# Low one-hots of a group's six chunks in two fixed buffers, in place of a ring addressed by register

## What is computed

```python
# layer 0: relational messages, summed by target node
Z = h @ W_shared.T; ze = he @ W_shared.T
a = Z[src] @ Wa_s.T + ze @ Wa_e.T + Z[dst] @ Wa_d.T
H_all = jnp.einsum('ni,rio->nro', h, W_rel)
out = relu(segment_sum(H_all[src, rel] * a, dst, N_NODES))
# layer 1 (twice) and layer 2 (four times): sums over the same edges
h = segment_sum(x[src], dst, num_nodes)
# layer 3: edge features summed by src, then an MLP
```

## Time and profile before

| what | us |
|---|---|
| median of 3 runs | 4683.87 (4682.92 to 4687.05) |
| the profiled execution, first to last instruction | 6104.5 |
| group stage in the profiled execution | about 226 to 3024 |
| from there to the end | about 3080 |

### The profile page before, as it was taken

The page is one execution under the profiler, slowest core; times in us unless marked ns, Lnnn a source line. Parts: engine busy times, 40 slices in busy tenths (PEclk is TensorE's granted clock), DMA queues, the critical chain, the costliest instruction groups (busy, mean ns, idle before and its releaser), DMA issues.

```text
span 6104.5 us, 83728 instructions
## 1 busy us (share of the span) xinstructions
PE 3504.6 (57%) x18191; PEld 1755.8 (29%) x18192; DVE 2563.8 (42%) x7891; ACT 1503.7 (25%) x3741; POOL 3187.4 (52%) x3191
## 2 busy tenths in 40 slices
PE   5377777777777777776324544345365345455347
PEld 2133333333333333333101222112132112222136
DVE  6266666666666666666330020131120021120368
ACT  3133333323323232322211111111111112111158
POOL 2455555555555555555376555645625635626720
PEclk8588888878888887888656676667666667667679
DMA  5333333333333333333123444334324334324256
GB/s 181 93 77 81 81 78 78 77 80 77 77 77 80 77 77 78 80 77 71 38 93 135 145 146 131 119 112 145 107 79 144 111 132 146 108 79 156 79 200 237
DMA packets 593641, 646.86 MB, mean 106 GB/s; under 512 B 423668, under 2 KB 430418, under 8 KB 587261
## 3 DMA queue, kind: packets, MB, share of 16 engines
q1 hardware_dynamic: 374705, 459.40, 23.2%
q0 software_dynamic: 101760, 110.75, 9.2%
q10 hardware_dynamic: 117068, 75.50, 4.1%
HBM read 451.74 MB, written 190.23 MB: 105 GB/s over the span
## 4 chain that ended last, share of the span: by engine, by line
PE 35%; issue 21%; another core or an unknown queue 21%; DVE 10%; DMA 8%; ACT 2%; POOL 2%; DVEq 1%; SPq 0%; ACTq 0%; POOLq 0%
PE bank L1742 10%; PE bank L1743 7%; PE bank L1823 6%; PE bank L1747 6%; DMA ld_all<-adjacency 3%; DMA rel_table<-ld_all 2%; DMA rel_and_z<-adjacency 1%; DVE hid_T L1305 1%; DMA ld_all<-l_sorted 1%; POOL l_sorted L711 1%; DVE hid_T L1326 1%; DVE hid_T L1584 1%; PE bank L1939 1%; PE bank L1771 1%
## 5 line engine op out<-in xcount | busy, mean ns | idle before, releaser
L711 POOL DMA_INDIRECT l_sorted<-arena,l_pos x1504 | 1539.2, 1023 | 1339.3 <-ACT arena L854 877.4
L686 POOL DMA_INDIRECT ld_all<-rel_table,rel_and_z x1564 | 1545.8, 988 | 1133.0 <-remote 503.2
L1742 PE MATMUL bank<-hid_T 128*128 128x400 f16 x2346 | 965.7, 412 | 672.6 <-issue 539.8
L1743 PE MATMUL bank<-hid_T 128*128 128x384 f16 x2346 | 940.5, 401 | 44.3 <-issue 43.5
L1326 DVE TENSOR_SCALAR hid_T<-count_key,hid_T 128x400 f16<-128x400 int16 x2346 | 592.1, 322 | 754.5 <-remote 526.7
L1823 PE MATMUL bank<-rel_and_z,ld_all 128*128 128x512 fp8e4 (+1 forms) x1872 | 522.3, 414 | 602.9 <-issue 534.1
L1823 PE MATMUL bank<-ld_all 128*128 128x512 fp8e4 (+1 forms) x1950 | 511.4, 420 | 337.4 <-issue 138.4
L1747 PE MATMUL bank<-ld_all,arena 128*32 x4692 | 527.1, 250 | 123.3 <-issue 121.3
L1742 PEld LDWEIGHTS bank<-hid_T 128*128 x2346 | 255.9, 109 | 1157.3 <-issue 1153.9
L774 ACT CAST ld_all<-bank 128x400 fp8e4<-128x400 f32 x391 | 191.1, 489 | 1551.6 <-remote 999.7
L1266 DVE COPY accT<-bank 128x512 f32<-128x512 f32 (+1 forms) x78 | 51.1, 656 | 1215.4 <-remote 797.1
(11 more groups left out here) (289 smaller groups left out, 4103.0 us busy)
## 6 DMA issues: line engine op xcount, KB each, us to landing
ld_all<-adjacency SPq DMA_DIRECT2D x72, 1600.0 KB
rel_and_z<-adjacency SPq DMA_DIRECT2D x72, 1600.0 KB
l_sorted<-zeros SPq DMA_DIRECT2D x147, 424.0 KB
arena<-in_edge_attr SPq DMA_DIRECT2D x195, 256.0 KB
ld_all<-l_sorted SPq DMA_DIRECT2D x33, 1277.5 KB, 6.0
adjacency<-ld_all ACTq DMA_DIRECT2D x391, 100.0 KB
rel_table<-ld_all SPq DMA_DIRECT2D x49, 520.0 KB, 3.6
ld_all<-rel_table,rel_and_z POOLq DMA_INDIRECT x1564
```

The costliest lines, as they stand in the source:

```text
L686: pool.indirect_dma_start(ring[:, c % RING, 0:TW], None, rel_table, bass.IndirectOffsetOnAxis(ap=rel_i[:, c:c + 1], axis=0)).then_inc(s(f" ...
L711: pool.indirect_dma_start(l3_sorted, bass.IndirectOffsetOnAxis(ap=l3_pos[0:parts, n * SB_K + k:n * SB_K + k + 1], axis=0), rows16[q][0:par ...
L1742: pe.matmul(b0[:, 0:w0], low[:, 0:P], pair_hot[q % 2][:, k, 0:w0], start=k == 0, stop=k == CG - 1)
L1743: pe.matmul(b1[:, 0:GW - w0], low[:, P:2 * P], pair_hot[q % 2][:, k, 0:GW - w0], start=k == 0, stop=k == CG - 1)
```

## The change

The ring goes. Two tiles `low_hot[0..1]` of six chunks each, and two small tiles of six keys each (`low_in`), take its place in `hid_T`. For each group DVE copies the six keys from `lo_key` at the group's first chunk (`low_keys`, an `also`, issued ahead of `pair_keys`), and makes six low one-hots from them (`low_hots`). PE takes `low_hot[q % 2][:, k, :]`, whose address is fixed when the program is compiled. The copy of 32 keys in each turn of the loop, the three rounds made ahead of the loop and the copy ahead of the tail go. The last three groups get low one-hots too, and their placeholder instruction is a memset of another tile.

```diff
-        lo_ring = hid_T[:, at:at + LO_RING * P].bitcast(f16).rearrange("p (c f) -> p c f", c=LO_RING)
-        assert at + LO_RING * P <= NP
+        low_hot, low_in = [], []
+        for q in range(2):
+            low_hot.append(hid_T[:, at:at + CG * P].bitcast(f16).rearrange("p (c f) -> p c f", c=CG))
+            at += CG * P
+            low_in.append(hid_T[:, at:at + CG])
+            at += CG
...
-                def low_hots(r, q, k0):
+                def low_keys(q, first):
+                    return v.tensor_copy(low_in[q % 2], lo_key[:, bass.ds(first, CG)])
+
+                def low_hots(q):
 
-                    for k in range(K):
-                        v.tensor_scalar(lo_ring[:, q * K + k, :], io256[:], lo_in[:, k0 + k:k0 + k + 1], None, ALU.is_equal)
+                    for k in range(CG):
+                        v.tensor_scalar(low_hot[q % 2][:, k, :], io256[:], low_in[q % 2][:, k:k + 1], None, ALU.is_equal)
...
-                link(v.tensor_copy(lo_in[:, 0:LAG * K], lo_key[:, 0:LAG * K]))
                 for r in range(LAG):
-                    low_hots(r, r, r * K)
                     link(add_source_term(r, r // 2, r % 2))
-                with fast.over(NG // TG, 2 + 4 + 2 * TG - 1 + 8) as b:
+                with fast.over(NG // TG, 2 + 4 + 3 * TG - 2 + 8) as b:
                     first = first_of(b * TG)
-                    fast.also(v.tensor_copy(lo_in, lo_key[:, bass.ds(b * (TG * K) + LAG * K, TG * K)]))
+                    fast.also(low_keys(0, first))
...
-                        low_hots(r, r % TG, q * K)
+                        low_hots(q)
...
+                            fast.also(low_keys(q + 1, coming))
                             link(pair_keys(g + 1, q + 1, coming))
...
                 for k in range(CG):
-                    low = lo_ring[:, bass.ds((first + k) & (LO_RING - 1), 1), :].rearrange("p a f -> p (a f)")
+                    low = low_hot[q % 2][:, k, :]
```

More of the change, by code:

```diff
@@ L294, in build @@
             at += CG
-        lo_ring = hid_T[:, at:at + LO_RING * P].bitcast(f16).rearrange("p (c f) -> p c f", c=LO_RING)
-        assert at + LO_RING * P <= NP
+        low_hot, low_in = [], []
[4 more added lines that the diff above has]
+            at += CG
+        assert at <= NP
         count_bank = [(4, 5), (0, 1)]
@@ L1396, in _ @@
                     positions(b)
-                link(v.tensor_copy(lo_in[:, 0:K * (ROUNDS % TG)], lo_key[:, ROUNDS // TG * TG * K + LAG * K:ROUNDS // TG * TG * K + LAG * K + K * (ROUNDS % TG)]))
                 v.wait_ge(s("he_loaded3"), 16 * (PIECES // 4) + 32)
@@ L1404, in _ @@
                     first = first_of(g)
+                    fast.also(low_keys(q, first))
                     link(pair_keys(g, q, first))
@@ L1407, in _ @@
                     row_hots(g, q, first)
+                    low_hots(q)
                     if r < ROUNDS:
-                        low_hots(r, r % TG, q * K)
                         link(add_source_term(r, r // 2, r % 2))
                     else:
-                        link(v.memset(lo_in[:, 0:1], 0))
+                        link(v.memset(over_sum[:], 0))
                     row_weights(q, first)
```

## The result

| | us | runs |
|---|---|---|
| before | 4683.4 (4680.37 to 4687.05) | 4 |
| after | 4911.6 (4908.57 to 4914.0) | 4 |

The ratio is 1.0488, 95% interval 1.0473 to 1.0503: the change makes the kernel 228 us slower. The forecast was 4657, in a range of 4590 to 4760. The result lies 152 us above its upper end, and no rival had named the cause.

What follows compares the result with a forecast made beforehand. PE's sequencer was taken to bind the group stage at 5.28 us a group; with DVE at 5.19 and POOL at 5.2 the pace becomes 5.21, so 391 x 0.07 = 27 us off 4683.87 gives 4657, range 4590 to 4760.

Steps and rivals of the forecast that it cites:

- DVE's turn: DVE's loop over eight groups: the turn itself takes 1.6 us, from the idle 1.07 ahead of L1370 to the first L1326.
- PE at 5.28 before: Group stage before the change: PE needs 5.28 us a group and its sequencer binds, read from a full-clock stretch.
- PE's chunks without addresses: PE at L1742: six chunks save 0.135 us each, 0.8 a group, and then follow each other by 0.33.
- DVE at 5.19: DVE in the group stage: two more one-hots and a key copy raise 4.74 to 5.19 us a group, between 5.1 and 5.3.
- POOL: POOL's gathers in the group stage: keep 5.0 to 5.2 us a group; six one-hots add 0.03 to 0.05; its wait vanishes.
- rival D: The port: each added one-hot holds POOL back for its whole 0.197 us, round 5.6, 125 us slower, 4809; 5%.
- Rival A: Group stage: PE's pace before was under 5.17, so DVE's 5.19 binds after; 74 or 35 us slower, 4758 or 4719; 27%.
- B: Group stage: POOL sets the pace before and after at 5.2, 0 to 9 us either way, 4684; 20%.
- C: Group stage: DVE and POOL are cheaper in a run, PE is not; 5.28 to 5.0, 109 us faster, 4575; 10%.
- The clock: PE's granted clock in the group stage: falling to half in places costs 0 to 15 us; taken as 0.
- The profiled span of 5450 to 5600: Profile after: with less PE sequencer work under the profiler, the span falls 500 to 660 us from 6104.5.
- Whole arrival: Group stage to end: later stages start behind it and POOL's long scatter is unchanged, so a gain there arrives whole.

Runs made afterwards that it cites:

- merged: The changed kernel with pair and low keys made by one instruction, so 287 instructions in a turn of DVE's loop in place of 303: 4652.1 us.
- merged_pad16: `merged` with 16 one-column memsets of an unused tile put into DVE's loop, 303 instructions a turn again: 4908.5 us.
- before_again: The kernel before, unchanged, profiled once more: a span of 4677.7 us, against 6104.5 in the first profile.
- pe_fixed: The kernel before with a fixed address for PE's low one-hots and DVE untouched, so the wrong chunks are read: 4666.2 us.
- full_unroll: The changed kernel with all 48 turns of DVE's loop written out, so no jump: 4629.4 us.
- pad16: The kernel before with 16 one-column memsets of an unused tile added to DVE's loop, 289 instructions a turn: 4671.4 us.
- two_turns: The changed kernel with DVE's loop body written twice, 24 turns of sixteen groups in place of 48 of eight: 4741.0 us.
- merged_unroll: `merged` with all turns of DVE's loop written out: 4656.3 us.
- before_unroll: The kernel before with DVE's loop of eight-group turns written out 48 times: 4679.9 us.

## Why the prediction was wrong

**The step that failed** is DVE's turn. The prediction carried it over unchanged ("the turn itself, from the idle 1.07 ahead of L1370 to the first L1326, 1.6") and said "No wait is added". It priced the added instructions by their execution and not by their place in the program. The term was 1.07 and became 6.43 a turn. 48 x 5.34 = 256 us, of which 28 are hidden or gained elsewhere; 228 were measured. No edit of the diff is the cause by itself: 16 memsets in the loop do it to `merged` (`merged_pad16`), and 32 ahead of it to the kernel before.

**PE at 5.28 before: right**, though read from an odd execution. A group takes 5.29 in `before_again`, PE is busy for 866 of 1000 us there at a clock of 0.97, and its weight loads at L1742 wait 380.6 us for "issue" in 1000. The stretch at full clock in the earlier trace rows was indeed what a run looks like.

**PE's chunks without addresses: right.** In after, timeline of PE at full clock:

```profile
1519.51 0.34 PE L1749 MATMUL bank<-hid_T 128*128 128x400 f16 x1 [1.17 <-DVE arena L1343]
1519.69 0.33 PE L1750 MATMUL bank<-hid_T 128*128 128x384 f16 x1
1519.85 0.33 PE L1749 MATMUL bank<-hid_T 128*128 128x400 f16 x1
```

Chunks follow each other by 0.34, against 0.49 and 0.46 in the earlier trace rows. What this is worth is another matter: `pe_fixed` has it alone, and gains 14 us.

**DVE at 5.19: near**, as what is left without the stall. 5.92 less 5.34 / 8 is 5.25, within the 5.1 to 5.3 of the prediction. `full_unroll`, which has no turn, makes a group in 5.18, and `merged`, which has no key copy, in 1000 / 192 = 5.21; DVE sets the groups' pace in both. `merged` takes 4652, close to the forecast of 4657, but that is in part luck: the forecast turns DVE's pace of 5.21 into time, and in `merged` POOL's gathers and scatters run through without a wait and set when the long scatter starts. The prediction had POOL's total (2113) and PE's (2114) a microsecond apart, so it saw how near POOL was.

**POOL: right.** Its round of 5.0 to 5.2 is the next bound in `pe_fixed`, and is 5.20 in `before_again`, 5.15 in `merged` and 5.10 in `full_unroll` from first to last gather. Six one-hots in place of four didn't slow a gather: 966 ns on average after, and 978 in `before_again`. POOL's wait for PE did not vanish, though; it grew to the 78.8 us shown above. The round of 5.10 to 5.15 with six one-hots excludes rival D's 5.6, and with it what the rule on the port in the Trainium skill's page SBUF — State Buffer, section "Who interferes with whom", gives when it is taken to the letter. Rival A's mechanism, PE's pace in a run under 5.17, is excluded by the 5.29. B and C named no loss of this size and fall with the result.

**The clock: right that it costs nothing here.** It falls from 0.97 to 0.86, as PE has waited longer between groups, and some groups go at 1.2 GHz: after the stall of 1498 us PE has waited 9.53 us, and its chunks then follow each other by 0.63.

```profile
1510.00 0.52 PE L1749 MATMUL bank<-hid_T 128*128 128x400 f16 x1 [9.53 <-DVE arena L1343]
1510.31 0.53 PE L1750 MATMUL bank<-hid_T 128*128 128x384 f16 x1
1510.63 0.54 PE L1749 MATMUL bank<-hid_T 128*128 128x400 f16 x1
```

In `full_unroll` the clock is 0.94 and DVE sets the pace all the same.

**The profiled span of 5450 to 5600: wrong.** It came from taking the 30% for something that the profiler does to PE's sequencer. A second execution of the same program had a span 1427 us shorter, so it belongs to that one execution. This also spoiled one of the prediction's signs: the median rose while the profiled span fell, which was to mean rival A, and A it was not.

**Whole arrival: right.** What the group stage loses arrives at the end. POOL's last gather moves from 2232 to 2465 us, and its long scatter starts 233 us later and takes 2084 us in after (2563.5 to 4647.8) and 2083 in `before_again` (2330.4 to 4413.5).

The range failed for a plain reason: it was made of bounds on durations, and held no case in which the program's own size costs something.

## What to carry to other kernels

Count the instructions from an engine's branch to the next, waits and register instructions included, before adding to a loop, and count only those (the code behind the loop isn't part of it). On DVE 273 to 303 were near the edge: 303 ran freely at two places, 273 stalled at a third, and a loop that stalled paid 3 to 5 us at each jump back. The sign is cheap to look for: many more packets on the instruction queue than the program has pieces, and "issue" idle time at the first instruction of each turn. Near the edge even unrelated code ahead of the loop moves the time by 4%, so compare two versions only once neither of them stalls, or write the loop out, which was the fastest here.

## What the hardware showed that I had not expected

- DVE's program came in packets of 8 KB (128 instructions), and a body that lay badly was read anew in each turn, 5 packets a turn, all or nothing: 67 packets or 303. Only the doubled and the written-out loops have other numbers (231 in `two_turns`, 151 in `full_unroll`, 145 in `merged_unroll`, 140 in `before_unroll`).
- The edge is sharp: a body that ended at 559 (`pad16`) idled 1.11 us at its jump, one that ended at 563 (`merged_pad16`) 6.42.
- Straight code cost no such wait: `full_unroll` streams 48 bodies, and the idle time ahead of a turn's first instruction is 14.3 us for 25 turns, less than with a loop that fits.
- A stalled DVE takes POOL with it although POOL is some 12 rounds of gathers ahead, for then the ring is full: 12 waits of up to 7.9 us in 600 us.
- One execution of an unchanged program was profiled at 6104.5 us and another at 4677.7, on one core. A span that is 30% from the runs should be taken again before it is explained.
